# Row order in a down product, a float16 query projection and parted bank copies in a perceiver kernel

## What is computed

```python
# first layer, feed-forward part, end
gate = act_qdq(gate * sig)
o = act_qdq(gate * up)                    # 512 x 1536, 16 bits
x = x + o @ lpbq_dequant(w_down).T        # the down product, 1536 -> 512
# second layer, cross attention, on q = layernorm(x), kv = context
qp = q @ Wq.T                             # the second query projection
scores = qp @ kv.T                        # 512 x 8192
idx = argmax(scores, axis=-1)
mem = kv[idx]                             # 512 rows of the context
mk, mv = split(mem @ Wkv.T)               # one key and one value head of 32
logits = einsum('hld,md->hlm', heads(qp, 16), mk) / sqrt(32)
out = softmax(logits) @ mv                # 16 heads over 512 remembered rows
x = x + merge(out) @ Wc.T
```

## Time and profile before

| what | us |
|---|---|
| median of 3 runs | 1106.28 |
| the three runs | 1106.1, 1106.28, 1110.31 |
| the profiled execution | 1104.84 |
| its span in the trace | 1103.1 |
| TensorE busy in the span | 1028.1 (93%) |
| VectorE, ScalarE, GpSimd busy | 820.7, 495.4, 417.0 |

### The profile page before, as it was taken

One profiled execution on the slowest core, in us unless ns is written; L12 is line 12 of the kernel. 1 busy time (PEld: TensorE's weight loads), 2 busy tenths in 40 slices (PEclk: granted clock), 3 DMA queues, 4 the chain that ended last, 5 costly groups with the idle time before them and its releaser, 6 DMA issues.

```text
span 1103.1 us, 14664 instructions
## 1 busy us (share of the span) xinstructions
PE 1028.1 (93%) x4907; PEld 483.4 (44%) x4907; DVE 820.7 (74%) x1176; ACT 495.4 (45%) x739; POOL 417.0 (38%) x228
## 2 busy tenths in 40 slices
PE   7999999999999989999929999999989889988997
PEld 3444444444444444544404444444452234466453
DVE  5566666799999557585974379999957787476896
ACT  2245545566666627415774211101036725356264
POOL 4287787400000363100002076776435743084003
PEclk9999999999999999899959999999999999999999
DMA  6145555623444056402001235445310020000001
GB/s 242 66 146 195 157 180 162 219 94 112 165 143 149 10 218 242 178 1 96 1 25 52 98 137 201 176 165 199 91 39 1 1 79 1 1 2 1 2 1 39
DMA packets 41831, 112.65 MB, mean 102 GB/s; under 512 B 4512, under 2 KB 15296, under 8 KB 35648
## 3 DMA queue, kind: packets, MB, share of 16 engines
q1 hardware_dynamic: 38592, 101.13, 26.1%
q10 hardware_dynamic: 2880, 9.96, 2.7%
q0 software_dynamic: 320, 1.05, 0.3%
HBM read 103.18 MB, written 7.34 MB: 100 GB/s over the span
## 4 chain that ended last, share of the span: by engine, by line
PE 79%; DVE 13%; ACT 4%; issue 2%; POOL 1%; DMA 1%; DVEq 0%; SPq 0%; ACTq 0%; POOLq 0%
PE PS L268 5%; PE PS L270 5%; PE PS L269 5%; PE PS L786 5%; PE PS L788 5%; PE PS L787 5%; PE PS L817 5%; PE PS L819 5%; PE PS L818 5%; PE PS L1727 5%; PE PS L1728 5%; PE PS L1729 5%; PE PS L262 2%; DVE arena L1652 2%; PE PS L758 1%
## 5 line engine op out<-in xcount | busy, mean ns | idle before, releaser
L786 PE MATMUL PS<-arena 128*128 128x512 f16 x256 | 97.0, 379 | 2.0 <-DVE arena L635 2.0
L1727 PE MATMUL PS<-arena 128*128 128x512 f16 x256 | 97.0, 379 | 1.9 <-DVE arena L1575 1.9
L817 PE MATMUL PS<-arena 128*128 128x512 f16 x256 | 97.0, 379 | 1.3 <-DVE arena L708 1.3
L787 PE MATMUL PS<-arena 128*128 128x512 f16 x256 | 97.0, 379 | 0.0
L788 PE MATMUL PS<-arena 128*128 128x512 f16 x256 | 97.0, 379 | 0.0
L1728 PE MATMUL PS<-arena 128*128 128x512 f16 x256 | 97.0, 379 | 0.0
L1729 PE MATMUL PS<-arena 128*128 128x512 f16 x256 | 97.0, 379 | 0.0
L818 PE MATMUL PS<-arena 128*128 128x512 f16 x256 | 97.0, 379 | 0.0
L819 PE MATMUL PS<-arena 128*128 128x512 f16 x256 | 97.0, 379 | 0.0
L642 DVE TENSOR_TENSOR arena<-PS,arena 128x512 f32<-128x512 f32 x64 | 43.6, 681 | 58.0 <-ACT arena L566 58.0
L500 POOL TENSOR_TENSOR arena<-arena 128x2048 f16<-128x2048 f32 x16 | 66.0, 4124 | 38.5 <-ACT arena L559 38.1
(11 more groups left out here) (389 smaller groups left out, 2416.7 us busy)
## 6 DMA issues: line engine op xcount, KB each, us to landing
arena<-in_ctxT SPq DMA_DIRECT2D x32, 1024.0 KB, 6.2
arena<-in_ctx SPq DMA_DIRECT2D x16, 1024.0 KB, 5.3
arena<-in_w ACTq DMA_DIRECT2D x8, 1024.0 KB, 5.3
arena<-in_w SPq DMA_DIRECT2D x8, 1024.0 KB, 6.6
XN<-in_ffnGU SPq DMA_DIRECT2D x16, 384.0 KB, 3.4
XN<-in_WinT SPq DMA_DIRECT2D x16, 290.0 KB, 5.0
gu_hi<-arena SPq DMA_DIRECT2D x16, 192.0 KB, 3.4
gu_lo<-arena SPq DMA_DIRECT2D x16, 192.0 KB, 3.5
```

Source lines behind the costliest of these rows:

```text
L786: pe.matmul(bank, CHI[:, b, e, cols], QHI[:, e, :], start=(e == 0), stop=False)
L787: pe.matmul(bank, CHI[:, b, e, cols], QLO[:, e, :], start=False, stop=False)
L817: pe.matmul(PS[:, t, :], PHI[:, j, cols], CHI[:, b, j, :], start=False, stop=False)
L1727: pe.matmul(bank, QHI3[:, e, cols], CHI3[:, b, e, :], start=(e == 0), stop=False)
```

## The change

Four edits come together.

- Down product: eight inner tiles are multiplied as before; after a wait for all twelve hidden tiles the last four (`BY_ROWS`) are multiplied row tile by row tile. The turns of rows 0 and 1 stand behind the products of rows 2 and 3. VectorE adds and normalises one row after the other (`add_tile`, `norm_tile`). Only five fillers are left, ahead of the last turn.
- Query projection: the weights are split into float16 halves ahead of it, scaled by `W_UP` = 64, by ScalarE (`WQ1_HI`) and VectorE (`WQ1_LO`) behind the hidden tiles; the turned rows are split with `split_x_act` and `split_x_dve`, as in other parts; the product is by `matmul_split`. The copies of the result undo the scale.
- Bank copies: the sums are copied after exponential 5, the values after exponential 7.
- Sums: for the last group GpSimd adds only tile 1; TensorE sums tile 2 and tile 3 itself. In `weighted` the float16 product is made first, from both float32 inputs, in place of the copy.

Counts of semaphores in `added` and in the `split_x_dve` calls of later parts follow.

```diff
+            act.wait_ge(w_in[3], 64)
+            act.activation(WQ1_HI, WQ1, ACT.Copy, scale=W_UP).then_inc(act_marks, 1)
             norm_act(act, 3)
...
-            add_and_norm(dve, 2, lambda t, ins: ins.then_inc(ln_xn, 1), scale=HUNIT)
+            dve.wait_ge(act_marks, ACT_MARK["s3_wq_hi"])
+            dve.scalar_tensor_tensor(out=WQ1_LO, in0=WQ1, scalar=W_UP, in1=WQ1_HI, op0=ALU.mult,
+                                     op1=ALU.subtract).then_inc(dve_marks, 1)
+            for t in range(NT):
+                add_tile(dve, 2, t, scale=HUNIT)
+                norm_tile(dve, 3, t).then_inc(ln_xn, 1)
...
-            for g in range(F0T):
+            for g in range(F0T - BY_ROWS):
                 pe.wait_ge(s2_hid, g + 1)
...
+                for t in range(NT):
+                    down(g, t)
+            pe.wait_ge(s2_hid, F0T)
             for t in range(NT):
-                fill(pe, 4 if t else 0, 8)
-                turn_tile(pe, 3, t)
+                for g in range(F0T - BY_ROWS, F0T):
+                    ins = down(g, t)
+                ins.then_inc(out_psum, 1)
+                if t >= 2:
+                    turn_tile(pe, 3, t - 2)
+            turn_tile(pe, 3, 2)
+            fill(pe, 4, 5)
+            turn_tile(pe, 3, 3)
...
-            return 8 * g + 4 * max(m - 1, 0) + j + 1
+            return 8 * g + 4 * max(min(m, 1 if g == GROUPS - 1 else 2) - 1, 0) + j + 1
...
-                if m in (0, NT - 1):
+                if m in (0, NT - 1) or (g == GROUPS - 1 and m == 2):
                     continue
...
-            transpose_x_act(act, 3)
+            split_x_act(act, 3)
             for e in range(DT):
                 act.wait_ge(s3_q_psum, e + 1)
-                act.copy(QHI3[:, e, :], PS[:, 4 + e, :]).then_inc(s3_q_hi, 1)
+                act.activation(QHI3[:, e, :], PS[:, 4 + e, :], ACT.Copy, scale=1.0 / W_UP).then_inc(s3_q_hi, 1)
...
-                if n % 16 == 6 and n > 16:
-                    take_group(n // 16 - 1)
+                if n % 16 == 5 and n > 16:
+                    take_sums(n // 16 - 1)
+                if n % 16 == 7 and n > 16:
+                    take_values(n // 16 - 1)
...
+            split_x_dve(dve, 2)
             for e in range(DT):
                 dve.wait_ge(s3_q_hi, e + 1)
-                dve.tensor_tensor(QLO3[:, e, :], PS[:, 4 + e, :], QHI3[:, e, :], ALU.subtract).then_inc(s3_q_lo, 1)
+                dve.scalar_tensor_tensor(out=QLO3[:, e, :], in0=PS[:, 4 + e, :], scalar=1.0 / W_UP, in1=QHI3[:, e, :],
+                                         op0=ALU.mult, op1=ALU.subtract).then_inc(s3_q_lo, 1)
...
+                dve.tensor_tensor(ATTT_HI[:, g, :], ATTT[:, g, :], DEN[:, g, :], ALU.mult).then_inc(s3_attt, 1)
+                dve.wait_ge(s3_attt, 4 * g + 2)
                 dve.tensor_tensor(ATTT[:, g, :], ATTT[:, g, :], DEN[:, g, :], ALU.mult).then_inc(s3_attt, 1)
-                dve.wait_ge(s3_attt, 4 * g + 2)
-                dve.tensor_copy(ATTT_HI[:, g, :], ATTT[:, g, :]).then_inc(s3_attt, 1)
...
-            pe.wait_ge(w_in[3], 64)
+            pe.wait_ge(dve_marks, DVE_MARK["s3_wq_lo"])
...
-                    ins = pe.matmul(PS[:, 4 + e, :], WQ1[:, c, e * P:(e + 1) * P], XT[:, c, :],
-                                    start=(c == 0), stop=(c == DT - 1))
+                    ins = matmul_split(pe, PS[:, 4 + e, :], (WQ1_HI[:, c, cols], WQ1_LO[:, c, cols]),
+                                       (XT_HI[:, c, :], XT_LO[:, c, :]), c, DT)
...
                 if n % 16 == 4 and 16 < n < UNITS:
-                    sums(n // 16 - 1)
+                    sums_added(n // 16 - 1, True)
+                    sums_tile(n // 16 - 1, NT - 1, stop=True)
                 if n >= 9 and n % 4 == 1:
                     weigh((n - 9) // 4)
-            sums(GROUPS - 1)
+                if n == UNITS + 2:
+                    sums_tile(GROUPS - 1, 2, start=True)
+                if n == UNITS + 4:
+                    sums_added(GROUPS - 1, False)
+            sums_tile(GROUPS - 1, NT - 1, stop=True)
```

More of the change, by code:

```diff
@@ L1036, in perceiver_kernel @@
         HUNIT = COLS[:, 30:31]
+        BY_ROWS = 4
         STEP = COLS[:, 31:32]
@@ L1312, in s2_pe, with down @@
             fill(pe, 0, 20)
-            for g in range(F0T):
+            def down(g, t):
+                w_hi, w_lo = DN_HI[:, g // GROUP, g % GROUP, :], DN_LO[g // GROUP][:, g % GROUP, :]
+                rows = slice(t * P, (t + 1) * P)
+                return matmul_split(pe, PS[:, 4 + t, :], (HID_HI[:, g, rows], HID_LO[:, g, rows]), (w_hi, w_lo), g, F0T)
+            for g in range(F0T - BY_ROWS):
                 pe.wait_ge(s2_hid, g + 1)
-                w_hi, w_lo = DN_HI[:, g // GROUP, g % GROUP, :], DN_LO[g // GROUP][:, g % GROUP, :]
                 for t in range(NT):
-                    rows = slice(t * P, (t + 1) * P)
-                    ins = matmul_split(pe, PS[:, 4 + t, :], (HID_HI[:, g, rows], HID_LO[:, g, rows]), (w_hi, w_lo), g, F0T)
-                    if g == F0T - 1:
-                        ins.then_inc(out_psum, 1)
+                    down(g, t)
+            pe.wait_ge(s2_hid, F0T)
             for t in range(NT):
-                fill(pe, 4 if t else 0, 8)
-                turn_tile(pe, 3, t)
+                for g in range(F0T - BY_ROWS, F0T):
[6 more added lines that the diff above has]
+            turn_tile(pe, 3, 3)
         W12B = view(53 * K, [8, 2048], F16)
@@ L1337, in perceiver_kernel @@
         SHIFT = view(146 * K, [DT, 2, N], F16)
+        WQ1_HI = view(146 * K, [DT, D], F16)
+        WQ1_LO = view(150 * K, [DT, D], F16)
         TRAW = view(154 * K, [2048])
@@ L1544, in shift_hi, with take_sums, take_values @@
                                scale=1.0 / MSHIFT).then_inc(s3_row_hi, 1)
-            def take_group(g):
+            def take_sums(g):
                 act.wait_ge(pe_marks, PE_MARK[f"s3_sums{g}"])
                 act.copy(DEN[:, g, :], PS[:, 7, :]).then_inc(s3_den, 1)
+            def take_values(g):
                 act.wait_ge(s3_pv, 4 * g + 4)
@@ L1820, in weigh, with sums_added, sums_tile @@
                 ins.then_inc(s3_pv, 1)
-            def sums(g):
+            def sums_added(g, start):
                 pe.wait_ge(s3_acc, added(16 * g + 11))
-                pe.wait_ge(s3_p, 16 * g + 16)
-                if g:
+                if g and start:
                     pe.wait_ge(s3_den, 2 * (g - 1) + 1)
                 for j in range(4):
-                    ins = pe.matmul(PS[DH * j:DH * (j + 1), 7, :], ONES[:, 0:DH], ACC[g % 2][:, j, :],
-                                    start=True, stop=False)
+                    pe.matmul(PS[DH * j:DH * (j + 1), 7, :], ONES[:, 0:DH], ACC[g % 2][:, j, :],
+                              start=start, stop=False)
+            def sums_tile(g, m, start=False, stop=False):
+                pe.wait_ge(s3_p, 16 * g + 4 * m + 4)
+                if start:
+                    pe.wait_ge(s3_den, 2 * (g - 1) + 1)
                 for j in range(4):
-                    ins = pe.matmul(PS[DH * j:DH * (j + 1), 7, :], ONES[:, 0:DH], PT[:, 12 + j, :],
-                                    start=False, stop=True)
-                ins.then_inc(pe_marks, 1)
+                    ins = pe.matmul(PS[DH * j:DH * (j + 1), 7, :], ONES[:, 0:DH], PT[:, 4 * m + j, :],
+                                    start=start, stop=stop)
+                if stop:
+                    ins.then_inc(pe_marks, 1)
             for e in range(FIRST):
@@ L2088, in s4_dve @@
         def s4_dve(dve, link):
-            split_x_dve(dve, 2)
+            split_x_dve(dve, 3)
             dve.wait_ge(small_in, 8 * 16)
@@ L2174, in s4_turned_lo @@
             def s4_turned_lo(q):
-                dve.wait_ge(xt_hi, 3 * DT + q + 1)
+                dve.wait_ge(xt_hi, 4 * DT + q + 1)
                 cols = slice(q * P, (q + 1) * P)
@@ L2385, in s5_dve @@
             dve.tensor_scalar(FCWS, FCW, W_MEAN[:, 0:1], None, ALU.mult).then_inc(dve_marks, 1)
-            split_x_dve(dve, 4)
+            split_x_dve(dve, 5)
             dve.wait_ge(dve_marks, DVE_MARK["s5_taps"])
```

5 lines of the change are left out of this document (3 added, 2 removed).

## The result

| what | before | after |
|---|---|---|
| median, us | 1106.19 (4 runs) | 1095.49 (4 runs, 1095.27 to 1097.87) |
| ratio | | 0.9902, 95% interval 0.9881 to 0.9923 |
| the profiled execution, us | 1104.84 | 1095.61 |
| its span, us | 1103.1 | 1093.9 |

A forecast was written before the change was run, and what follows sets the result against it. Bound: a chain through all engines before the TensorE-filled scores loop, and latencies between logits and exponentials behind it. 5.4 - 0.8 + 3.4 = 8.0, plus 1.0 + 0.2 + 1.4 = 2.6, gave 10.6 us gained: 1095.6 us, range 1092.5 to 1099.5.

The forecast's parts named there:

- Down product: Before the scores loop: finishing row by row brings the last row's transposes from 618.45 to 613.0, 5.4 us gained.
- Hand-over: From transposes to the first query matmul: splitting the turned rows takes 1.82 us instead of 1.04, 0.8 us lost.
- projection: Second query projection: 48 float16 matmuls instead of 16 in float32 take 10.57 us instead of 14.01, 3.4 us gained.
- The weights' split: Ahead of the query projection: new work on ScalarE and VectorE, hidden with 5 us to spare; uncovered it would cost 4.2.
- Rival 2: Scores loop: the earlier start is not carried through; only 2.6 us remain, 1103.7 us; chance 0.08.
- Parted copies: Second attention, group starts: copying sums and values apart gains 1.0 us at the first place, about 0.2 at the second.
- The last group: End of the second attention: TensorE bounds once GpSimd's last four adds go; VectorE is ready earlier; 1.4 us gained.
- one of the prediction's own signs of being wrong: End of the second attention: early output rows waiting on VectorE's last difference would show the forecast wrong; no size given.
- Rival 1: Second attention: VectorE and GpSimd hold each other up, 1.40 us per block; 8.0 us remain, 1098.2 us; chance 0.14.
- Rival 3: TensorE's clock falls near the last transposes: short, 1097.6 us, chance 0.05; long into the scores loop, 1110.6, chance 0.03.
- Rival 4: Whole change: more gained, 3.4 us for the attention and 9 for the rest, 1093.8 us or lower; chance 0.10.

The follow-up runs named there:

- e1_rows: The kernel before with only the down product's new order and the rows added and normalised one behind the other: 1100.15 us, ratio 0.9943.
- e4_fill: The kernel before without the eight fillers ahead of the last turn of the normalised rows, nothing else: 1103.98 us, ratio 0.9976.
- e2_proj: The kernel before with only the query projection in float16 halves: 1102.93 us, ratio 0.9970.
- e7_nopart: The changed kernel with both bank copies after exponential 6 again: 1099.41 us, ratio 0.9938.
- e5_cast: The changed kernel with the old order in VectorE's three attention blocks, float32 product and then a cast: 1092.77 us, ratio 0.9895.
- e6_nosums: The changed kernel with GpSimd adding the last group's tile 2 again and all sums behind the last weighing: 1099.22 us, ratio 0.9936.
- e12_sums: The changed kernel with the last group's old sums, GpSimd's next-part memset and mask later and two fillers instead of ten: 1094.84 us, ratio 0.9892.
- e11_shift: The changed kernel with 34 fillers instead of 20 ahead of the down product: 1097.96 us, ratio 0.9917.
- e9_best: The changed kernel with float32 product then cast, GpSimd's next-part memset and mask later, and two fillers instead of ten: 1092.47 us, ratio 0.9881.

## Why the prediction was right

**Down product, 5.4 forecast.** Right: from first matmul to last turn 34.6 us (577.57 to 612.15) against 40.0, and e1_rows alone gained 5.4. The rows came 2.7 to 2.8 us apart, not 2.65, because the add entered 0.03 to 0.09 us before the end of the row before it and not 0.15; the turn was forecast for 613.0 and stood at 613.0 when counted from the old start (612.15 + 0.88). The five fillers delayed nothing. e4_fill adds what the prediction did not part: 1.6 of it are eight fillers.

**Hand-over 0.8 lost, projection 3.4 gained.** Right: 1.83 us from the last turn to the first matmul (1.82 forecast), 10.55 to the last copy (10.57), and 2.8 by e2_proj alone. The weights' split was hidden, by 5.6 us (5 forecast).

**Through the scores loop.** Rival 2 is refuted: the loop took 165.1 us, and TensorE was busy 165.00 of 165 with VectorE at 153.36.

**Parted copies, 1.0 and 0.2.** The first place gave 0.98. The second was mis-sized: 0.45, since the sums of group 2 still wait for GpSimd, but its adds moved further than the prediction gave them. Together 1.4, and e7_nopart says 1.4.

**The last group, 1.4.** This is the step that failed, though the sum hides it. In the prediction's words, "A product written straight into float16 in place of the cast saves 1.38 - 0.75 = 0.63 each". That sets a cast held up by GpSimd against a product that was not. In before, the three products of the earlier trace rows took 0.69, 0.70 and 0.85 because the add that ran when each began had only 0.13, 0.16 and 0.30 us left. The next adds waited for them and took 1.75, 1.63 and 1.71 us in place of 1.27, and the casts waited for these adds. The first block in before shows it (L1668 is the product, L1511 GpSimd's add, L1670 the cast):

```profile
872.98 0.69 DVE L1668 TENSOR_TENSOR arena<-arena 128x512 f32<-128x512 f32 x1
873.06 1.75 POOL L1511 TENSOR_TENSOR arena<-arena 128x512 f32<-128x512 f32 x1
873.71 1.38 DVE L1670 CAST arena<-arena 128x512 f16<-128x512 f32 x1
```

The 1.40 that the prediction gave an add was a mean too, over 1.28, 1.28 and 1.75. Like against like, the exchange costs 0.26 each, as e5_cast showed. So VectorE's three blocks took 19.4 us in after (859.29 to 878.69) against 19.6 in before, 0.2 saved where 1.9 were forecast, and 18.7 with the cast. VectorE should have ended at 886.1, with the sums at 887.7 behind it. Counted from the first weighing as before (8.86 later than the times of after), VectorE ended at 887.5 and the sums near 877.01 + 1.04 + 8.86 = 886.9. The forecast time of the end, 887.7, was met (878.83 + 8.86), by the other engine: one of the prediction's own signs of being wrong, a wait of the early output rows on VectorE's last difference, is there with 0.78 us. What the last group's edits gave is, less the 1.4 of the copies, 1.0 of the 2.4 us in after, in place of 1.4, and 1.7 of the 3.1 in e5_cast.

**Rival 1** came in part. VectorE did end the attention, for 0.7 us (e5_cast) and not for 4.2. But the holding up was nothing new: by the single instructions it lengthened VectorE's products, casts and differences by 4.0 us in before, 3.0 in after and 3.1 in e5_cast, and the 0.7 are the product's own price. The Trainium skill's page "SBUF — State Buffer" (section "SBUF: two separate sides") says that a VectorE operation with two SBUF inputs and a GpSimd operation that reads SBUF exclude each other and that the loser waits for the whole instruction. The trace agrees in kind: the product from 869.27 ended at 870.83, 0.55 us behind the end of GpSimd's add from 869.02 (870.28). What the rule was taken to say here, that the attention's part would come to nothing, did not come: 2.4 us are left.

**Rival 3** came in its short form, at a place that the prediction had not named: after loses 1.4 us in the next part by a clock that falls behind the same 2.56 us of waiting that before went through at full speed. The prediction had held the waits of the changed stretch for the danger; there the clock did fall in e6_nosums and e12_sums (1.6 us each), but not in after.

**The sum.** 8.2 + 2.4 = 10.6 in the two stretches, as forecast, and that is luck in part: 0.7 lost to VectorE nearly cancelled 0.2 more than forecast ahead of the scores, 0.25 more at the second place and some 0.3 more at the sums. Rival 4's larger gain did not come. The medians differ by 10.7; the profiled executions by 9.2, which is these 10.6 less 1.4 for the clock, plus 0.9 and less 0.6 in code that wasn't touched and less 0.2 around the scores loop. The prediction's 1094.2 for a profiled execution was therefore 1.4 short of the 1095.61 measured, and the 1.44 that it added for the median made up for that by luck.

## What to carry to other kernels

Where a product's row tiles all finish with its last inner tile, finishing them one by one lets the next stage's chain run beside the rest of the product; it was worth 5.4 us here, of which 1.6 were only fillers standing ahead of work that had become ready. When one VectorE instruction is exchanged for another beside a busy GpSimd, compare both alone, or both held up, by single rows and not by means: here a cast took 0.43 or 1.38 us and the product in its place 0.69 or 1.65, and the held cast against the free product made a loss look like a gain. Look also whether GpSimd's own work can wait: moving a memset and a mask, and dropping fillers, gave a further 0.6 and 1.7 us in the next part. After a gain, look at which engine ends the stretch now, even when the total came out as forecast.

## What the runs showed of the hardware

The granted clock fell behind short waits, and not always behind the same ones. A wait of 2.56 us left it at 1.00 in before and e11_shift and was followed by 0.50 in after; 2.29 us ahead of the last sums left it at 1.00 in before and were followed by 0.50 in e2_proj; 0.95 and 1.16 us of waiting left it at 1.00 in after, and 0.94 and 1.17 were followed by half speed in e6_nosums and e12_sums, where the same code began within 0.2 us of the same time. Each fall cost 1.1 to 2.8 us. The spread within one kernel goes with it, as far as the mean clock of each run shows: e5_cast's runs with 0.987 took 1092.4 to 1092.8 us, those with 0.983 and 0.978 took 1097.1 and 1098.0. What decides whether it falls stays open; a shift of the start (e11_shift) moved it away in one profiled execution, which is no rule.

VectorE was held up by GpSimd in one-input operations too: the float32 row of 128 x 512 took 0.55 us alone, 1.18 beside a memset and 2.06 beside a mask, and the cast to float16 0.43 alone (876.54 in e9_best) and 1.38 or 1.39 beside adds. A product of two inputs was held for about as long as the add that ran when it began had still to go, less some 0.14 us: it took 0.69 us with 0.13 us left (872.98 in before), 0.91 with 0.36 left and 1.56 with 1.01 left (862.66 and 869.27 in after). An add that came behind a product was held in turn: behind the product from 868.99 in e5_cast, which kept its 0.69 us, it took 1.80 in place of 1.27.
